# Another order of steps in the two long attentions of a four-layer kernel

## The reference

```
# layer 0: attention 1, 8 heads of 16 channels, 1024 positions
qkv  = einsum('oc,bchw->bohw', qkv_w, x) + qkv_b
attn = softmax(einsum('bhcn,bhcm->bhnm', q, k) * 128**-0.5)
out  = einsum('bhnm,bhcm->bhcn', attn, v)
x    = x + proj_w @ out + proj_b
# layer 1: whitening and colouring of the channels in groups of 16
# layer 2: group norm, a small convolution as gate, then attention 2:
standard_out = softmax(qh @ kh.T / 4) @ vh            # 8 heads of 16 channels
for wq, wk, wv in two sets:                           # 2 heads of 64 channels
    parts.append(softmax(qm @ km.T / 8) @ vm)
fused = silu([standard_out, parts] @ ff_w1.T + b) @ ff_w2.T + b ...
# layer 3: gamma * softmax(q.T @ k) v + x, one head, 16 channels of q and k
```

## Time and profile before

| | us |
|---|---|
| median of 3 runs | 5059.58 (5055.86 to 5066.26) |
| the profiled execution | 5058.94, its span 5057.1 |
| busy: PE, DVE, ACT, POOL | 4349.9 (86%), 3754.8 (74%), 3109.4 (61%), 1615.1 (32%) |
| attention 1, first to last values | about 117 to 1566 |
| attention 2, first to last values | about 2211 to 4376 |

### The profile page before, as it was taken

The page is one execution under the profiler, slowest core; times in us unless marked ns, Lnnn a source line. Parts: engine busy times, 40 slices in busy tenths (PEclk is TensorE's granted clock), DMA queues, the critical chain, the costliest instruction groups (busy, mean ns, idle before and its releaser), DMA issues. The chain is left out here.

```text
span 5057.1 us, 70342 instructions
## 1 busy us (share of the span) xinstructions
PE 4349.9 (86%) x26130; PEld 1312.9 (26%) x26130; DVE 3754.8 (74%) x4271; ACT 3109.4 (61%) x5549; POOL 1615.1 (32%) x894
## 2 busy tenths in 40 slices
PE   3999999899996666479999999999999999678888
PEld 1222222222223621112222222222222222223332
DVE  6999988999992357677777777777777777268774
ACT  1888887887885123246676666777766667434444
POOL 1111111111100011214444444333444443336666
PEclk7999999999998977679999999999999999879999
DMA  2212212222112023221111011111111110111211
GB/s 61 49 41 67 50 47 62 46 58 56 41 37 75 26 96 115 81 48 41 39 35 39 24 42 43 43 44 41 43 43 43 41 31 14 35 59 60 67 65 53
DMA packets 140179, 253.57 MB, mean 50 GB/s; under 512 B 56144, under 2 KB 56144, under 8 KB 139728
## 3 DMA queue, kind: packets, MB, share of 16 engines
q1 hardware_dynamic: 139856, 249.28, 18.1%
HBM read 155.20 MB, written 85.13 MB: 48 GB/s over the span
## 5 line engine op out<-in xcount | busy, mean ns | idle before, releaser
L640 DVE TENSOR_REDUCE c_mx<-banks 128x2 f32<-128x1024 f32 x1280 | 1536.0, 1222 | 534.6 <-PE banks L452 334.3
L545 ACT ACTIVATE c_e<-banks 128x512 f32<-128x512 f32 x2560 | 1387.7, 594 | 685.0 <-PE banks L478 327.0
L640 DVE TENSOR_REDUCE a_mx<-banks 128x2 f32<-128x1024 f32 x1024 | 1220.2, 1221 | 156.9 <-PE banks L444 143.2
L545 ACT ACTIVATE a_e<-banks 128x512 f32<-128x512 f32 x2048 | 1110.8, 594 | 252.9 <-PE banks L468 234.1
L493 PE MATMUL banks<-a_e,a_vs 128*32 128x512 f32 x4096 | 557.9, 617 | 0.2 <-ACT a_e L545 0.2
L493 PE MATMUL banks<-c_e,c_vs 128*32 128x512 f32 x4096 | 546.2, 605 | 0.0
L395 POOL TENSOR_TENSOR c_esum<-c_e,c_esum 128x1024 f32<-128x1024 f32 x224 | 527.0, 2353 | 41.5 <-ACT c_e L545 22.1
L444 PE MATMUL banks<-a_stack 48*128 48x512 f16 x2048 | 392.3, 394 | 107.7 <-DVE a_mx L640 66.7
L444 PE MATMUL banks<-c_stack 48*128 48x512 f16 x2048 | 385.1, 393 | 87.4 <-DVE c_mx L640 65.7
L468 PE MATMUL banks<-a_stack 50*128 50x512 f16 x2048 | 404.5, 392 | 45.6 <-ACT a_e L545 41.9
L468 PE MATMUL banks<-c_stack 50*128 50x512 f16 x2048 | 398.4, 386 | 23.8 <-ACT c_e L545 17.0
(11 more groups left out here) (315 smaller groups left out, 4945.7 us busy)
## 6 DMA issues: line engine op xcount, KB each, us to landing
a_stack<-q_halves SPq DMA_DIRECT2D x96, 128.0 KB, 3.4
a_stack<-k_halves SPq DMA_DIRECT2D x96, 128.0 KB, 6.8
c_stack<-q_halves SPq DMA_DIRECT2D x96, 128.0 KB, 4.5
c_stack<-k_halves SPq DMA_DIRECT2D x96, 128.0 KB, 5.9
a_res<-in_x SPq DMA_DIRECT2D x16, 512.0 KB, 4.1
a_xin<-in_x SPq DMA_DIRECT2D x16, 512.0 KB, 4.5
q_halves<-a_parts SPq DMA_DIRECT2D x16, 512.0 KB, 3.0
k_halves<-a_parts SPq DMA_DIRECT2D x16, 512.0 KB, 2.8
```

Source lines behind the costliest of these rows:

```text
L545: nc.scalar.activation(e[q % 4][:, 2 * i + h, :], bank_of(n - 1 + h), ACT.Exp).then_inc(st_free, 1)
L640: nc.vector.tensor_reduce(mx[j % 2][:, :, i, qc, half], slot[:, :, :], AX.X, ALU.max).then_inc(mr_free, 1)
```

## The change

The numbers of the timetable go into two tables, `TIMES` for attention 1 and `TIMES_MIXED` for attention 2, and pieces get a start, a step and an offset each instead of one common offset of 0.7. No instruction is added or taken away.

```diff
-    SCORE, VALUES, PIECE, EVAC, SCORE2, MAXIMA, MAXIMA2 = 0.05, 0.2, 0.7, 0.38, 0.45, 0.6, 0.8
-    begin = 1 if mixed else -5
+TIMES = {
+    "score": 0.05, "pv": 0.2, "evac": 0.38, "score2": 0.45, "max": 0.02, "max2": 0.6, "begin": -5, "qk": (0, 1, 0.7), "v": (7, 1, 0.25),
+    "vd": (0, 1, 0.7), "dqk": (0, 1, 0.7), "done": 9, "proj": (0, 1, 0.25), "turn": (0, 1, 0.25), "dsum": (0, 1, 0.7),
+    "bound": (0, 1, 0.25), "esum": 0.06}
+TIMES_MIXED = {
+    "score": 0.15, "pv": 0.33, "evac": 0.88, "score2": 0.47, "max": 0.01, "max2": 0.32, "begin": 12, "qk": (-5, 1, 0.93), "v": (6, 1, 0.3),
+    "vd": (0, 2, 0.51), "dqk": (16, 1, 0.77), "done": 25, "proj": (0, 1, 0.77), "turn": (0, 1, 0.69), "dsum": (-2, 1, 0.3),
+    "bound": (0, 1, 0.51), "esum": 0.94}
...
-        piece = lambda slot, *step: add(slot + PIECE, *step)
+        piece = lambda slot, i, *step: add(slot + A[step[0]][0] + A[step[0]][1] * i + A[step[0]][2], *step)
...
-            piece(ahead + begin + i, "qk", b, i // 2, i % 2)
+            piece(ahead + begin, i, "qk", b, i // 2, i % 2)
...
-            piece(ahead + (begin + 4 if mixed else 2) + i, "v", b, i)
+            piece(ahead + begin, i, "v", b, i)
...
-            add(first - LEAD + 0.70, "turn", b, g)
+            add(first - LEAD + A["turn"][0] + A["turn"][2], "turn", b, g)
...
-        done = start + size + (13 if mixed else 9)
+        done = start + size + A["done"]
```

More of the change, by code:

```diff
@@ L85, in timetable @@
     add = lambda time, *step: at.append((time, len(at), step))
-    SCORE, VALUES, PIECE, EVAC, SCORE2, MAXIMA, MAXIMA2 = 0.05, 0.2, 0.7, 0.38, 0.45, 0.6, 0.8
-    begin = 1 if mixed else -5
+    A = TIMES_MIXED if mixed else TIMES
+    SCORE, VALUES, EVAC, SCORE2, MAXIMA, MAXIMA2 = A["score"], A["pv"], A["evac"], A["score2"], A["max"], A["max2"]
+    begin = A["begin"]
     for b in range(NB):
@@ L90, in timetable @@
         ahead = start - size
-        piece = lambda slot, *step: add(slot + PIECE, *step)
-        add(ahead - size + begin + 12.5 if mixed else ahead - size + 4.5, "load", b)
+        piece = lambda slot, i, *step: add(slot + A[step[0]][0] + A[step[0]][1] * i + A[step[0]][2], *step)
+        add(ahead - size + begin + max(A[k][0] + A[k][1] * n + 0.98 for k, n in (("qk", 3), ("v", 1), ("dqk", 3 * mixed), ("vd", mixed))), "load", b)
         if b == 0 or not mixed:
             add(ahead + begin - 4 + 0.9, "reach", b)
-            piece(ahead + begin - 3, "bound", b)
-            add(ahead + begin - 3 + 0.71, "ratio", b)
+            piece(ahead + begin - 3, 0, "bound", b)
+            add(ahead + begin - 3 + A["bound"][2] + 0.005, "ratio", b)
             add(ahead + begin - 1.5, "scales", b)
         for i in range(4):
-            piece(ahead + begin + i, "qk", b, i // 2, i % 2)
-        add(ahead + begin + 3.95, "split", b)
-        add(ahead + begin + 6.5, "stackstore", b)
+            piece(ahead + begin, i, "qk", b, i // 2, i % 2)
+        ready = ahead + begin + A["qk"][1] * 3
+        add(ready + 0.95, "split", b)
+        add(ready + 3.5, "stackstore", b)
         for i in range(6):
-            add(ahead + begin + 8.5 + i, "stackload", b, i)
+            add(ready + 5.5 + i, "stackload", b, i)
         for i in range(2):
-            piece(ahead + (begin + 4 if mixed else 2) + i, "v", b, i)
+            piece(ahead + begin, i, "v", b, i)
         if mixed:
             for i in range(2):
-                piece(ahead + begin + 6 + i, "vd", b, i)
+                piece(ahead + begin, i, "vd", b, i)
             for i in range(4):
-                piece(ahead + begin + 8 + i, "dqk", b, i // 2, i % 2)
-            add(ahead + begin + 12, "dsplit", b)
+                piece(ahead + begin, i, "dqk", b, i // 2, i % 2)
+            add(ahead + begin + A["dqk"][0] + A["dqk"][1] * 3 + 1, "dsplit", b)
         for g, group in enumerate(groups):
@@ L129, in timetable @@
                     else:
-                        add(slot + SCORE + 0.01, "esum", b, g, half, kc)
+                        add(slot + A["esum"], "esum", b, g, half, kc)
                     add(slot + 2 + VALUES, "pv", b, g, half, kc)
@@ L134, in timetable @@
             if group.kind == "D":
-                piece(done + 2, "dsum", b, g)
+                piece(done + 2, 0, "dsum", b, g)
                 done += 3
@@ L141, in timetable @@
             add(done + 4.7, "norm", b, g)
-        done = start + size + (13 if mixed else 9)
+        done = start + size + A["done"]
         for i in range(4):
-            piece(done + i, "proj", b, i)
-        add(done + 3.9, "store", b)
-        add(done + 3.9, "residual", b + 1)
+            piece(done, i, "proj", b, i)
+        add(done + A["proj"][1] * 3 + 0.9, "store", b)
+        add(done + A["proj"][1] * 3 + 0.9, "residual", b + 1)
     return [step for _, _, step in sorted(at)]
```

## The result

| | before | after |
|---|---|---|
| median of 12 runs, us | 5061.53 (5055.86 to 5085.77) | 5040.80 (5022.33 to 5049.05) |
| profiled execution, its span | 5058.94, 5057.1 | 5036.08, 5034.3 |

What follows compares the result with a forecast made beforehand. Loops between TensorE and ScalarE and through VectorE, plus TensorE's own order in attention 2, bound the kernel. 5058.9 - 29 (attention 1) - 27 (attention 2) = 5003, median 5004 us; forecast 4992 to 5016, range 4982 to 5036.

Steps and rivals of the forecast that it cites:

- Projection slots: Attention 1: piece inside the loop with ScalarE, 3.45 us against 3.47; nothing taken for six slots, bounds +-10 us in all.
- transposition: Attention 1: VectorE then sets the slot, about 3.0 us in place of 3.53, a gain of 0.55.
- the one among the q and k pieces: Attention 1: transposition slot falls from 3.53 us to the ordinary 3.13 plus 0.27, a gain of 0.14.
- The two slots with `v`: Attention 1: piece inside the ScalarE loop, 2.39 + 1.06 = 3.45 us; a loss or gain of 0.1 allowed.
- At the bound: Attention 1: three slots fall from a mean of 11.0 to 9.7 us without the clock drop; 19 us over 14 images.
- Rival 1: Attention 1: half clock stays at `bound`, 16 us less gain, 5020; chance 0.17.
- The cycle of a slot without a piece is unchanged ..., so 2.39 stays.: Attention 1: slots without a piece keep their order of second score, two pairs, first score, values, at 2.39 us.
- plain S slots: Attention 2, S scores with S pairs, no piece: second pair inside the loop, 2.61 us where it was 2.39; seven slots.
- wide slots: Attention 2, wide heads: score between the pairs ends a wait for VectorE; 2.40 us from 2.52, gaining 1.9 an image.
- a wait of 0.97 at `dsum`: Attention 2: TensorE waits 0.9 us for GpSimd's last sum of exponentials; 135.0 remain of 137.0 an image.
- rivals 2 and 3: Attention 2: half clock from the `dsum` wait, 5024, chance 0.13; `dsum` much too early, slower, 5098, chance 0.07.
- The later `evac` ... would cost 0.5 ..., but each of those has a piece after it ...: nothing: Attention 2: copy behind the second score's exponentials in slots 1, 9, 17 and 25, covered by following pieces, costs nothing.

Runs made afterwards that it cites:

- e3: Kernel after plus unread full-width products in slots 14 to 31 of attention 1's last image; 5021.8 us, ratio 0.9907.
- e1: New timetable for attention 1 only, old numbers for attention 2; 5041.9 us, ratio 0.9948 against the kernel before.
- e8: Kernel after plus unread products in attention 1's last image, each 2 columns wide instead of 512; 5031.5 us, ratio 0.9927.
- e5: On top of e3, attention 1's `reach` one slot earlier in VectorE's queue; 5018.9 us, ratio 0.9899.
- e12: On top of e7 with `dsum` one slot later, every copy of attention 2 ahead of the second score's exponentials; 4989.3 us, ratio 0.9836.
- e7: On top of e3, both pairs together ahead of the first score in attention 2's S slots; 4993.0 us, ratio 0.9853.
- e10: Kernel after without fill, copies in attention 1's last image moved behind the second score's exponentials; 5022.4 us, ratio 0.9917.

## Why the prediction was off

**Attention 1, images 0 to 14: right, by half for another reason.** Projection slots of 3.45 (forecast 3.45), transposition 2.96 (2.98), the one among the q and k pieces 3.39 (3.40), and -27.0 us for the forecast -29. The two slots with `v` take 3.55 where 3.45 was counted, within the 0.1 a slot that was allowed. At the bound the sum was right (9.72 for 9.7 on average) and the parts were not. The clock was forecast to stay up there; it still falls in eight images of fourteen. It costs 0.7 now and not 1.33, and the slots without it take 9.3, less than the 9.7 of my count of VectorE's work. Rival 1, the half clock that stays, came in part and cost 8 x 0.7 = 6 us; with 16 us it had overpriced the drop. That the total is right is luck to that extent.

**The step that failed: "The cycle of a slot without a piece is unchanged ..., so 2.39 stays."** It was read from an image in the middle and multiplied by fifteen; the last image, in which 19 of 32 slots have no pairs at all, was not looked at. There TensorE was busy 23.84 of 33 us before, at full clock. The rivals placed half clock at `bound` and at `dsum`, both at pauses, and none where TensorE has too little to do. There it can fall and stay down to the end of the attention: 18 us in the profiled execution, and 19 between the medians of the kernel after and e3. That is half of the 37 us between forecast and result; the rest is 9 in attention 2, 4 between the attentions, 2 in attention 1, and the 4.7 by which the median lies above the profiled execution, where 0.6 was taken.

The order in those slots did not change, and the half clock is not new. By time, 26 of 73 executions of the kernel before took 5076 to 5089 and the rest 5073 or less (where the clock is on record, 0.935 to 0.939 and 0.940 or more); of the kernel after it was eleven of twelve. Whether the new order meets it more often is open: e1, with the very same attention 1, had it in five of twelve, hardly more than the kernel before, and its last image starts as early as that of after (1462.4 and 1461.1, before 1487.7). By the Trainium skill, "TensorE: Matmul & The Clock Gate", section "What's actually happening", the hardware's look at activity is not tied to the start of the program, so that the number of slow products at the start of one kernel differs from run to run. Here the two groups of four in e8 show two outcomes of one kernel 1500 us behind its start.

**Between the attentions: +4.2 us, left out of the sum.** The prediction had nothing for this stretch. It took between 646.1 and 652.1 us in the profiled executions. Two things move it. One is the half clock around 1650 to 1680 us, in work whose order no kernel changed: it lasts 10.2 us in the executions with 646.6, 646.9 and 647.5, and 27.3 or 34.1 in those with 650.8, 649.0, 649.3 and 652.1; e5, with 20.5 and 646.1, does not fit. The other is the run-up of attention 2, from its first q and k piece to its first values, where the new table does change the order: 81.8 to 83.1 us in the three executions with the old table and 83.1 to 85.1 in the eleven with the new one. In the pair before and after, 1.5 of the 4.2 us lie ahead of that piece and 2.7 behind it.

**Attention 2: the order of sizes right, the gain mis-sized.** Slot by slot it is close: plain S slots 2.61 (2.61), `vd` 3.38 (3.33), projection 3.78 (3.76), wide slots 2.41 (2.40), no half clock, a wait of 0.97 at `dsum` (0.9); rivals 2 and 3 did not come. The usual image is 135.6 for 135.0, and the fourteen middle ones gained 1.4 each and not 2.0. The largest single part is the term "The later `evac` ... would cost 0.5 ..., but each of those has a piece after it ...: nothing". A q and k piece behind a copy waits itself: 3.37 for 3.13, 0.24 an image, as e12 shows by taking it away. The slot of `dsum` and the wide heads' slots as a whole took 0.2 each more than counted, the other pieces 0.02 to 0.05 each; the two slots in which `dqk` stands with a projection piece and with the transposition took 7.6 for 8.0. The forecast took 3 us off the 30 for the first image and for VectorE. In fact the first and the last image of attention 2 took 0.5 and 0.8 longer than before; the first varied from 128.8 to 136.4 us over the profiled executions, so its part is not to be put down to the order.

**The range** reached to 5036. The last image alone, 18 to 19 us, would have brought 5004 to 5023, above the forecast of 5016 and inside the range. It took the other parts as well, the 9 of attention 2 above all, to leave it; and without the last image they too would have stayed inside.

**Where half of the gain of attention 2 lay.** The 2.61 of the plain slots was counted and accepted as part of the change. e7 shows that it was not needed: the new order pays in the wide slots, where a pair would wait for VectorE, and costs in the S slots, where the pairs lie in the shadow of the exponentials.

## What to carry to other kernels

Count the ends of a loop apart from its middle: here the work ahead had run out, TensorE's granted clock fell in a part of the executions, and unread products in its free time made the kernel faster. A wait taken away tells its worth only in a run, since the next one often stands right behind it: 1.0 at `dsum` was worth 0.6, and the copy that stood behind it 0.5 more. Of a wait with several semaphores, look at what ended just before it, not at the name; and an order that helps in one kind of slot is to be tried in that kind alone.

## What the runs showed of the hardware

In after TensorE stayed at 1.2 GHz for 51 us (e8: 55) although it was idle for at most 0.94 us at a time before the drop and 0.72 us within it, and its slots took 3.70 us for 2.39: in both traces the half clock, once there, held until the attention was at its last values. With the same instructions in the same order, 20.81 us busy of 29.3 at full clock, e1 ran through at 2.4 GHz, and so did e10 with 20.01. So the same load carried both levels. By time and mean clock, eleven of twelve executions of after and five of twelve of e1 had the low one; what decides it is open. With the fill of full width TensorE was busy 26.02 us of 29.3, and the seven traces have full clock there.
